# A graph network kernel gathers rows of x and searches the edge lists inside its loop instead of building a node table first

## What is computed

```
h = x @ w_lin + b_lin
msg = h[edge_src]                                    # 400,000 rows
dense = zeros(n, 32, 64).at[edge_dst, pos].set(msg)  # pos: place of an edge among its node's
xb = _mab(dense, dense, enc...)                      # 32 x 32 attention per node, masked
xp = relu(xb @ pma_lin_w + pma_lin_b)
p  = _mab(seed, xp, pma...)                          # one query per node over its 32 slots
dd = _mab(p, p, dec...)
out = layernorm(x + relu(nan_to_num(dd)))
# _mab: q, k, v by in_w, in_b; softmax(q k / 8) v; h = o @ out_w + out_b + x; h + relu(h @ ff_w + ff_b)
```

## Time and profile before

| what | value |
|---|---|
| median of 3 runs | 4282.87 us (4282.56 to 4283.9) |
| the profiled execution, its own time | 4279.91 us |
| its span in the profile | 4278.1 us |
| PE busy | 3488.9 us, 82% |
| POOL busy | 3155.2 us, 74% |
| DVE busy | 2677.3 us, 63% |
| ACT busy | 1391.3 us, 33% |
| granted PE clock, mean | 0.955 |
| gathers of the loop | 3136, the first at 275.4 us, the last at 4196.0 us |

### The profile page before, as it was taken

How to read it: one execution, slowest core, us unless ns; L and a number is a source line. 1 busy time by engine, 2 the same in 40 slices (tenths; PEclk the granted TensorE clock), 3 DMA queues, 4 the chain that set the end, 5 groups by cost and what they waited for, 6 DMA issues and landing times.

```text
span 4278.1 us, 111348 instructions
## 1 busy us (share of the span) xinstructions
PE 3488.9 (82%) x43804; PEld 2153.5 (50%) x43804; DVE 2677.3 (63%) x5467; ACT 1391.3 (33%) x2596; POOL 3155.2 (74%) x3353
## 2 busy tenths in 40 slices
PE   3716888888888888888888888888888888888887
PEld 1414555555555555555555555555555555555554
DVE  6744566666666666666666666666666666666665
ACT  0202333333333333333333333333333333333332
POOL 5777777777777777777777777777777777777771
PEclk9999999999999999999999999999999999999998
DMA  5633222222222222222222222222222222222230
GB/s 156 198 104 75 55 54 54 54 54 55 54 55 55 54 55 54 54 55 54 54 54 54 55 54 55 54 55 55 54 55 55 54 55 54 54 55 54 57 77 17
DMA packets 166583, 264.92 MB, mean 62 GB/s; under 512 B 95221, under 2 KB 109526, under 8 KB 166102
## 3 DMA queue, kind: packets, MB, share of 16 engines
q0 software_dynamic: 111328, 239.45, 21.0%
q1 hardware_dynamic: 54806, 18.27, 1.9%
HBM read 247.88 MB, written 11.23 MB: 61 GB/s over the span
## 4 chain that ended last, share of the span: by engine, by line
POOL 55%; issue 24%; PE 14%; DMA 5%; DVE 2%; POOLq 1%; ACT 0%; ACTq 0%; DVEq 0%
POOL gathered L578 52%; DMA gathered<-node_table,idx 3%; PE ps L688 3%; PE ps L651 3%; PE ps L669 2%; PE ps L704 2%; PE ps L723 1%; POOL xp_rows L544 1%; PE ps L753 1%; POOL gathered L544 1%; PE ps L727 1%; PE ps L763 1%; PE ps L745 1%; DVE hT L883 0%; POOLq L113 0%
## 5 line engine op out<-in xcount | busy, mean ns | idle before, releaser
L578 POOL DMA_INDIRECT gathered<-node_table,idx x3136 | 2966.1, 946 | 955.8 <-issue 939.0
L651 PE MATMUL ps<-ident,gathered 128*128 128x128 f32 x3136 | 526.1, 317 | 539.0 <-DMA gathered<-node_table,idx 538.4
L1071 DVE SCALAR_TENSOR_TENSOR xb<-ps,cols,h 128x512 f32<-128x512 f32 x392 | 294.3, 751 | 1020.4 <-PE ps L723 1020.2
L651 PEld LDWEIGHTS ps<-ident,gathered 128*128 128x128 f32 x3136 | 439.8, 211 | 633.5 <-issue 430.8
L772 ACT ACTIVATE xp_rows<-ps 128x512 f32<-128x512 f32 x392 | 234.1, 597 | 1184.2 <-PE ps L745 1184.2
L772 ACT ACTIVATE qT<-ps 128x512 f32<-128x512 f32 x392 | 234.1, 597 | 1052.3 <-PE ps L651 1052.3
L1126 DVE STREAM_TRANSPOSE probs_diag<-probs 32x512 f32<-32x512 f32 x784 | 550.9, 703 | 29.0
L669 PE MATMUL ps<-xb,pma_diag 128*128 128x512 f32 x784 | 478.6, 697 | 0.0
L688 PE MATMUL ps<-probs_diag,gathered 128*64 128x128 f32 x6272 | 454.9, 290 | 0.3 <-DVE h L993 0.3
L688 PEld LDWEIGHTS ps<-probs_diag,gathered 128*64 128x64 f32 x6272 | 359.1, 145 | 179.3 <-issue 169.5
L723 PE MATMUL ps<-h,ff_diag 128*128 128x512 f32 x784 | 440.7, 644 | 0.8 <-ACT xp L813 0.4
(11 more groups left out here) (184 smaller groups left out, 3324.2 us busy)
## 6 DMA issues: line engine op xcount, KB each, us to landing
gathered<-node_table,idx POOLq DMA_INDIRECT x3136
node_table<-hT SPq DMA_DIRECT2D x14, 448.0 KB, 4.4
qT<-in_x SPq DMA_DIRECT2D x13, 224.0 KB, 5.4
rows<-in_x SPq DMA_DIRECT2D x24, 112.0 KB
out_rows<-rows SPq DMA_DIRECT2D x20, 104.0 KB
gathered<-in_dst,win_idx POOLq DMA_INDIRECT x98, 4.2
xp_rows<-src_padded,sidx POOLq DMA_INDIRECT x98
src_padded<-in_src SPq DMA_DIRECT2D x1, 1562.5 KB, 15.9
```

What stands on the lines that cost most here:

```text
L578: pool.indirect_dma_start(out=gathered[:, s.slot(0, RING), t * ROW:(t + 1) * ROW], out_offset=None, in_=table, in_offset=bass.IndirectOffs ...
L651: mm = pe.transpose(ps[:, bank, p * P:(p + 1) * P], gathered[:, s.slot(0, RING), lo:lo + 2 * ROW - 1:2], ident[:, :])
L1071: V.scalar_tensor_tensor(xb[:, s.slot(L_FF, 2), :], ps[:, B_FF, :], c_("ff_b", P), h2[:, s.slot(L_FF, 2), :], ALU.add, ALU.max).then_inc(x ...
```

## The change

The node table is gone. POOL gathers rows of x itself, 64 numbers or 256 bytes each. PE makes 4 transposes of them per octet; the ACT copy gives xT. One step later PE multiplies xT by `q_diag` (a new 512-column matmul), which gives the queries, and the scores use xT as keys. The product with w_lin reaches h2 through a second new 512-column matmul per octet, `lin_diag` with xT, which starts the sum in the bank that the output matmul ends. The bias moves into constants.

The search moves into the loop. At the start SP writes a table of 1,250 rows to device memory; each holds 352 values of dst and 352 of src, from one sample on. For each iteration DVE counts its nodes against the 1,250 samples (`rows_of`, eleven octets ahead, on step 1), POOL gathers one row of 704 numbers per node (six octets ahead, on its step 2), and DVE then finds start and count in it (`search`, five octets ahead, at the end of step 3): two counts over 352, a handful of small operations, and 9 predicated copies that shift the src part down by the bits of the start. PE adds two small matmuls per iteration for the counts. The last octet of 392 has no node and is left out, as are 3 gathers of the one before it; row numbers are no longer copied per octet.

```diff
 EPS = 1e-5
 
-SAMPLES = 625
-HALF = 7
-CHUNK = 7
-
-
+SAMPLES = 1250
+SAMPLE_TILES = 10
...
-    OCTETS = ITS * OCTS_PER_IT
-    WINDOW = E // SAMPLES
-    CHUNKS = ITS // CHUNK
-    assert x.shape[1] == D and SAMPLES * WINDOW == E and ITS % (2 * HALF) == 0 and ITS % (2 * CHUNK) == 0
-    SEARCHES = ITS // HALF
+    OCTETS = -(-N // (QUADS * OCT))
+    STRIDE = E // SAMPLES
+    WIN = STRIDE + DEG
+    assert x.shape[1] == D and SAMPLES * STRIDE == E and STRIDE % DEG == 0 and WIN < 512 and ITS % 2 == 0
+    SAMPLE_ROWS = SAMPLES // SAMPLE_TILES
+    assert (SAMPLES - 1) // 16 * 16 == SAMPLES - 2
+    BITS = 9
+
...
+            for c, edges in enumerate((dst, src)):
+                sp.dma_start(win_table[0:whole, c * WIN:(c + 1) * WIN],
+                             bass.AP(tensor=edges.tensor, offset=0, ap=[[STRIDE, whole], [1, WIN]])
+                             ).then_inc(table_in, 16)
+                sp.dma_start(win_table[whole:SAMPLES, c * WIN:(c + 1) * WIN],
+                             bass.AP(tensor=edges.tensor, offset=whole * STRIDE, ap=[[E - WIN - whole * STRIDE, 2], [1, WIN]])
+                             ).then_inc(table_in, 16)
...
-            pool.wait_ge(tab_out[1], 16 * (CHUNKS // 2))
+            def gather_windows(u, h, ready):
+                ready(win_idx_ready, u + 1)
+                pool.indirect_dma_start(
+                    out=windows[:, h, 0:2 * WIN], out_offset=None, in_=win_table,
+                    in_offset=bass.IndirectOffsetOnAxis(ap=win_idx[:, h:h + 1], axis=0)).then_inc(win_in[h], 16)
+
+            pool.wait_ge(table_in, 64)
+            for u in range(AHEAD):
+                gather_windows(u, u, pool.wait_ge)
...
+                if s.has_iteration(-6) and (s.looped or s.at >= 2):
+                    u = s.iteration(-6)
+                    wait_apart(pool, idx_ready, u - 1, pool_passed)
+                    gather_windows(u, s.slot(-6, RING) // OCTS_PER_IT,
+                                   lambda sem_, count_: wait_apart(pool, sem_, count_, pool_passed))
                 wait_apart(pool, av_ps, s.octet(RING - 1), pool_passed)
-                wait_apart(pool, idx_ready, s.octet(-1), pool_passed)
-                for t in range(OCT):
+                if s.has_iteration(0):
+                    wait_apart(pool, idx_ready, s.iteration(0) + 1, pool_passed)
+                first = s.slot(0, RING) * OCT
+                for t in range(tiles_of(s.octet(0))):
                     pool.indirect_dma_start(
-                        out=gathered[:, s.slot(0, RING), t * ROW:(t + 1) * ROW], out_offset=None, in_=table,
-                        in_offset=bass.IndirectOffsetOnAxis(ap=idx[:, s.slot(0, RING), t:t + 1], axis=0),
+                        out=gathered[:, s.slot(0, RING), t * D:(t + 1) * D], out_offset=None, in_=x,
+                        in_offset=bass.IndirectOffsetOnAxis(
+                            ap=idx[:, first // DEG, first % DEG + t:first % DEG + t + 1], axis=0),
                     ).then_inc(g_in[s.slot(0, RING)], 16)
 
...
 
-                    wait(pe, q_sb, s.octet(0))
-                    pe.wait_ge(g_in[s.slot(0, RING)], s.round(0) * (16 * OCT) + 16 * OCT)
-                    turn(s, 0, B_Q).then_inc(q_ps, 1)
-
+                    wait(pe, x_sb, s.octet(0))
+                    landed = tiles_of(s.octet(0))
+                    if landed:
+                        pe.wait_ge(g_in[s.slot(0, RING)], s.round(0) * (16 * OCT) + 16 * landed)
+                    for p in range(PAIRS):
+                        mm = pe.transpose(ps[:, B_Q, p * P:(p + 1) * P],
+                                          gathered[:, s.slot(0, RING), p * P:(p + 1) * P], ident[:, :])
+                    mm.then_inc(x_ps, 1)
+                if s.has(L_Q):
                     if s.has(L_BACK + 1):
                         wait(pe, back_sb, s.octet(L_BACK))
                     else:
-                        wait(pe, h_sb, s.octet(0))
-                    turn(s, 1, B_HX).then_inc(h_ps, 1)
+                        wait(pe, q_sb, s.octet(L_Q))
+                    wait(pe, x_sb, s.octet(L_Q - 1))
+                    pe.matmul(ps[:, B_HX, :], q_diag[:, :], xT[:, s.slot(L_Q, RING), :], start=True, stop=True
+                              ).then_inc(q_ps, 1)
                 if s.has(L_PMA):
                     wait(pe, xb_sb, s.octet(L_PMA - 1))
                     pe.matmul(ps[:, B_FF, :], pma_diag[:, :], xb[:, s.slot(L_PMA, 2), :], start=True, stop=True
@@ -684,17 +578,22 @@
                     wait(pe, h2_sb, s.octet(L_ATTEND))
...
-                    wait(pe, q_sb, s.octet(L_SCORES - 2))
-                    wait_apart(pe, h_sb, s.octet(L_SCORES - 2), pe_passed)
+                    wait_apart(pe, q_sb, s.octet(L_SCORES - 2), pe_passed)
+                    if s.has_iteration(L_SCORES):
+                        m = s.iteration(L_SCORES)
+                        wait_apart(pe, count_ok, m + 1, pe_passed)
+                        par = s.slot(L_SCORES, RING) // OCTS_PER_IT
+                        pe.matmul(ps_counts[:, 0:QUADS], fold, count_quad[:, par, :], start=True, stop=True)
+                        pe.matmul(ps_counts[:, QUADS:QUADS + 1], pool_perm, count[:, par, :], start=True, stop=True)
...
-                    pe.matmul(ps[:, B_AV, :], vo_diag[:, :], avT[:, s.slot(L_ATTEND, 2), :], start=True, stop=True
+                    pe.matmul(ps[:, B_AV, :], lin_diag[:, :], xT[:, s.slot(L_ATTEND, RING), :], start=True, stop=False)
+                    pe.matmul(ps[:, B_AV, :], vo_diag[:, :], avT[:, s.slot(L_ATTEND, 2), :], start=False, stop=True
                               ).then_inc(vo_ps, 1)
...
                 if s.has(0):
-                    act.wait_ge(q_ps, s.octet(-1))
-                    wait(act, s_ps, s.batch(4) + 1)
-                    copy(qT[:, s.slot(0, 4), :], ps[:, B_Q, :]).then_inc(q_sb, 1)
-                    act.wait_ge(h_ps, s.octet(-1))
-                    wait(act, h2_sb, s.octet(RING - 1))
-                    copy(hT[:, s.slot(0, RING), :], ps[:, B_HX, :]).then_inc(h_sb, 1)
+                    act.wait_ge(x_ps, s.octet(-1))
+                    wait(act, vo_ps, s.octet(RING - 1))
+                    copy(xT[:, s.slot(0, RING), :], ps[:, B_Q, :]).then_inc(x_sb, 1)
+                if s.has(L_Q):
+                    act.wait_ge(q_ps, s.octet(L_Q - 1))
+                    wait(act, s_ps, s.batch(L_Q + 4) + 1)
+                    nc.scalar.activation(qT[:, s.slot(L_Q, 4), :], ps[:, B_HX, :], ACT.Identity, bias=c_("q_b", P)
+                                         ).then_inc(q_sb, 1)
...
+            def rows_of(u, h):
+
+                V.tensor_scalar(flags[0][:, :], samples[:, :], node_f[:, bass.ds(u, 1)], None, ALU.is_lt, ALU.add,
+                                accum_out=win_row[:, h:h + 1]).then_inc(sampled, 1)
+                dve.wait_ge(sampled, u + 1)
+                V.tensor_scalar(win_idx[:, h:h + 1], win_row[:, h:h + 1], -1.0, None, ALU.add
+                                ).then_inc(win_idx_ready, 1)
+
+            def search(u, h, rounds):
+
+                dve.wait_ge(win_in[h], rounds * 16 + 16)
+                dst_win = windows[:, h, 0:WIN]
+                src_win = windows[:, h, WIN:2 * WIN + DEG]
+                node = node_f[:, bass.ds(u, 1)]
+                V.tensor_scalar(flags[1][:, :], dst_win, node, None, ALU.is_lt, ALU.add, accum_out=below[:, :]
+                                ).then_inc(found, 1)
+                V.tensor_scalar(flags[2][:, :], dst_win, node, None, ALU.is_le, ALU.add, accum_out=upto[:, :]
+                                ).then_inc(found, 1)
+                dve.wait_ge(found, u * 2 + 2)
+                V.tensor_copy(below_i[:, :], below[:, :]).then_inc(found_int, 1)
+                V.tensor_scalar(count[:, h, :], upto[:, :], below[:, :], float(DEG), ALU.subtract, ALU.min
+                                ).then_inc(found_int, 1)
+                dve.wait_ge(found_int, u * 2 + 2)
+                V.tensor_tensor(below_bits[:, :], below_i[:, :].broadcast_to((P, BITS)), bit_of[:, :], ALU.bitwise_and
+                                ).then_inc(bits_ok, 1)
+                V.tensor_scalar(count_quad[:, h, :], quad_of[:, :], count[:, h, :], None, ALU.mult).then_inc(count_ok, 1)
+                V.transpose(count_turned[:, :], count[:, h, :].broadcast_to((P, DEG))).then_inc(bits_ok, 1)
+                wait_apart(dve, bits_ok, u * 2 + 2, dve_passed)
+                V.tensor_copy(count_slot[:, bass.ds(u * DEG, DEG)], count_turned[:, :])
+                for b in reversed(range(BITS)):
+                    far = min((1 << b) - 1, WIN - (1 << b)) + DEG
+                    V.copy_predicated(src_win[:, 0:far], below_bits[:, b:b + 1].broadcast_to((P, far)),
+                                      src_win[:, 1 << b:(1 << b) + far]).then_inc(shifted, 1)
+                    wait_apart(dve, shifted, u * BITS + (BITS - b), dve_passed)
```

(38 more changed lines are left out.)

488 lines of the change are left out of this document (163 added, 325 removed).

## The result

The changed kernel takes 4540.7 us (median of 4, 4532.1 to 4556.3) against 4283.4 beside it (4 runs): a ratio of 1.0604, 95% interval 1.0574 to 1.0634. So it is 6% slower, where 4558 us had been forecast. The profiled run took 4532.1 us, with a span of 4529.9.

What follows compares the result with a forecast made beforehand. POOL's gathers bound the old kernel; afterwards PE's circle through DVE's search would: 44.1 + 1.0 clock = 45.1 us, 137 + 97.7 iterations x 45.1 = 4543, adjusted to a span of 4553 and time of 4558 us; range 4165 to 4760.

Steps and rivals of the forecast that it cites:

- Outside of the gathers: Time before the first and after the last row gather: 50 + 82 + 5 = 137 us instead of 357.5.
- POOL: Gathers: row length doesn't matter, 944 ns each; 33 per iteration take 41.3 us; waits for attention products about 3 us.
- The search: DVE's search at the end of step 3, ahead of h2: 6.2 us, with bounds of 4.4 and 7.4.
- rival 2: Low bounds meet: search of 4.4 us, clock doesn't fall; circle 42.3 us, time about 4275 us; chance 0.08.
- The stall: PE stands still before step 0's attention products, waiting for DVE's h2: 4.1 us per iteration.
- The second stall: PE waits again before the scores of step 0: under 1 us; both stalls together 4.9 us.
- B: Rest of PE's iteration, from step 0's attention products to the next step 3's ff: 33.1 us without the clock.
- The clock: PE's clock falls after the stall and slows the operations behind it: 1.0 us added per iteration.
- rival 1: Gathers still set the pace, if the circle stays under 41.3 us: 4168 us; chance 0.18.
- Rival 3: Clock falls at every stall and the search is at its upper end: 37.9 + 7.4 + 2.5 = 47.8, 4807 us; chance 0.07.
- S: Length of DVE's search, taken as 6.2 us; the circle lasts 37.9 + S = 44.1 us.
- Rival 4: The search on DVE slows POOL's gathers: an iteration of 49.2 us on POOL, 4944 us in all; chance 0.04.

Runs made afterwards that it cites:

- e6_split: Changed kernel with the search cut in two: counts in step 3 ahead of xb, copies and transpose in step 0 ahead of xb; 4155.8 us, ratio 0.9714.
- g3_double: Changed kernel with nine more predicated copies on a scratch tile chained behind the search's nine; 4841.2 us, ratio 1.1286.
- g4_nolin: Changed kernel without the lin_diag matmul, one 512-column matmul per octet; 4183.6 us, ratio 0.9763.
- e5_warm: Changed kernel with four unread 512-column matmuls on PE in step 0, ahead of its wait for h2; 4392.4 us, ratio 1.0264.

## Why the prediction was right

The time came out 17 us under the forecast, within the range, and by the mechanism forecast: h2 behind the search, one stall of about 4 us per iteration, and the clock behind it. That the time fits so closely is partly luck, since errors of up to 0.6 us an iteration (59 us in all) cancel. Point by point:

**Outside of the gathers.** Forecast 137 us, measured 32.9 + (4529.9 - 4427.2) = 135.6, as two errors that cancel. The first row gather starts at 32.9 us, not 50, and outside the range given for it (35 to 70); the part behind the last gather is 102.7 instead of 87.

**POOL.** The gathers of the narrower rows take 945 ns (944 forecast), and an iteration of 33 costs 41.26 us where POOL is free to run (e6_split; 41.3 forecast). It waits 2.9 us an iteration for the attention products; about 3 had been forecast.

**The search.** 5.9 us against 6.2. The nine copies with their gaps take 3.47 us (g3_double) against 4.0; a copy has a mean of 240 ns, 2.16 us for the nine as forecast (9 x 0.17 + 0.64), so what was too large is the gap behind a separate wait: 0.15 us (line 804), not 0.20. The low bound of rival 2, 4.4, was far from it.

**The stall.** 4.25 us in the mean against 4.1, released by h2. A, from ff to the attention products, was forecast as 4.8 + 6.2 = 11.0 us and is 10.9, whether PE has one matmul less there (g4_nolin) or four more (e5_warm). The second stall, 0.8 us at the scores, shows only where the clock stays up (0.87 in e5_warm); in the changed kernel PE at half clock fills the same time.

**The rest of the circle.** B was forecast as 44.1 - 11.0 = 33.1 us without the clock, and PE's 512-column matmuls follow at 0.86 us (2035.61 to 2036.46), not at the 0.95 that I took from the group ahead of them. In e5_warm, with the clock up, B is 32.4 to 32.7 us in 10 of the 14 circles that I read (2012.39 to 2045.02 is 32.63), and 34.2 to 35.6 in the other four; in the one of 35.4 I found a stop of 1.2 us by "issue" in the scores, and behind it the granted clock is 0.50 from 2212 to 2214 us, with the stall filled as everywhere. In the changed kernel the waits name 13.0 us of such stops in 22 iterations, 0.6 us each, which I had not counted: 0.34 inside ff, 0.25 in the scores.

**The clock.** Priced at 1.0 us. What e5_warm takes away is 1.4 to 1.5, of which about 0.95 is the clock and about 0.45 the stops inside ff. So the price was right, though for the wrong operations, and the stops were missing from the sum: I had counted transposes, the attention products and the matmul behind them. Attention products and scores pay nothing, since DVE's probs hold PE there anyway; ff, lin and vo behind them pay it. The mean granted clock of 0.933 lies at the lower edge of the forecast 0.93 to 0.98.

So 45.0 us measured against 45.1 forecast is 10.9 + 32.5 + 1.4, plus 0.2 of stops in the scores (those inside ff are in the 1.4), where I had 11.0 + 33.1 + 1.0. B was 0.6 too long without the clock, and 0.6 of aftermath and stops was missing: these two cancel. The rivals: rival 1 (the gathers set the pace, 4168 us) is what e6_split does, at 4155.8, once the search leaves the path; its condition was wrong for this order of DVE's work, its price right to 12 us. Rival 3 had the clock fall at every stall, and in all 14 circles it did; but S stayed at 5.9 instead of 7.4 and the clock cost 0.95 instead of 2.5. Rival 4 (the search slows the gathers) is out by the 944 and 945 ns.

## What to carry to other kernels

Work added to an engine that is a third idle can cost nearly its full length (3.1 of 3.5 us in g3_double) if the engine that sets the pace waits for what is queued behind it: price it by the stretch from the last input to the next output that someone waits for, not by the busy share. The same search cost 381 us more of the whole time ahead of h2 (0.089 x 4283) than in two stretches ahead of xb where DVE was waiting anyway; look for the idle stretches of the engine before choosing a place. A repeated stall of TensorE had a second price behind it here, 1.4 us an iteration, and it was paid only by the operations that nothing else held back.
